# First layer of a two-layer fusion kernel: the value projection of two batches and four skip products change their place in TensorE's order

## The reference, cut to what matters

```python
def _L0_tok_ref(x, w_qkv, b_qkv, w_out, b_out):      # 16 heads of 16
    q, k, v = jnp.split(qkv, 3, axis=-1)
    logits = jnp.einsum('bhqd,bhkd->bhqk', q, k) / math.sqrt(HEAD_DIM)
    attn = jax.nn.softmax(logits, axis=-1)
    vals = jnp.einsum('bhqk,bhkd->bhqd', attn, v)
...
def _L0_attn_ref(u, A_log, D_skip, dt_proj_w, dt_proj_b, x_proj_w):   # 16 states, 589 tokens
    delta = jax.nn.softplus(jnp.einsum('blr,dr->bld', dlow, dt_proj_w) + dt_proj_b)
    h = dA * h + dB * u_t[..., None]
    y_t = jnp.sum(h * c_t[:, None, :], axis=-1)
...
    return y + u * D_skip[None, None, :]
```

## Time and profile before

| | us |
|---|---|
| median of 3 runs | 1267.5 |
| lowest and highest of them | 1264.88, 1269.35 |
| the profiled execution | 1260.33 |
| its span, first to last instruction | 1258.1 |
| share of PE, DVE, ACT, POOL busy in the span | 77%, 60%, 35%, 14% |

### The profile page before, as it was taken

One profiled execution on the slowest core, in us unless ns is written; L12 is line 12 of the kernel. 1 busy time (PEld: TensorE's weight loads), 2 busy tenths in 40 slices (PEclk: granted clock), 3 DMA queues, 4 the chain that ended last, 5 costly groups with the idle time before them and its releaser, 6 DMA issues.

```text
span 1258.1 us, 14643 instructions
## 1 busy us (share of the span) xinstructions
PE 974.3 (77%) x4854; PEld 531.5 (42%) x4855; DVE 760.9 (60%) x1321; ACT 444.4 (35%) x816; POOL 170.0 (14%) x200
## 2 busy tenths in 40 slices
PE   6999888888978889897685429998199887638880
PEld 2323332243322434234352229997066665414440
DVE  4611689975799768988799721111555657742225
ACT  1165236632366422674452113443123312302220
POOL 1000000000000000000000612333000023245550
PEclk9799899997999989899788759999599989769995
DMA  3099302300223102122233386663650000239927
GB/s 97 1 299 309 126 33 96 117 20 11 74 84 119 41 3 78 58 98 76 89 116 107 101 331 204 192 201 98 226 231 1 6 18 14 70 101 396 401 90 246
DMA packets 74058, 156.58 MB, mean 124 GB/s; under 512 B 11194, under 2 KB 55437, under 8 KB 70928
## 3 DMA queue, kind: packets, MB, share of 16 engines
q1 hardware_dynamic: 66512, 148.11, 34.5%
q0 software_dynamic: 7488, 7.70, 1.9%
HBM read 124.88 MB, written 43.69 MB: 134 GB/s over the span
## 4 chain that ended last, share of the span: by engine, by line
PE 44%; DVE 29%; issue 15%; DMA 3%; POOL 3%; ACT 3%; SPq 1%; another core or an unknown queue 1%; POOLq 0%; DVEq 0%; ACTq 0%
DVE hst L1534 10%; PE ps L594 7%; PE ps L1065 5%; DVE hC L1542 5%; PE ps L572 4%; PE ps L678 4%; PE ps L700 3%; PE ps L943 3%; DVE mxn L1483 3%; PE ps L1053 2%; PE ps L691 2%; PE ps L1013 2%; POOL ys_dram L1441 2%; PE ps L582 1%; DVE Hs L2058 1%
## 5 line engine op out<-in xcount | busy, mean ns | idle before, releaser
L700 PE MATMUL ps<-hC,ident 128*128 128x512 f32 (+1 forms) x384 | 158.1, 553 | 49.4 <-DVE hC L1542 49.4
L1483 DVE TENSOR_REDUCE mxn<-ps 128x2 f32<-128x1024 f32 x128 | 151.1, 1221 | 68.2 <-PE ps L594 67.8
L1534 DVE TENSOR_TENSOR_SCAN hst<-dA,dBu 128x1180 f32<-128x1180 f32 x64 | 167.0, 2610 | 0.5
L1145 ACT ACTIVATE Ph<-ps 128x1024 f32<-128x1024 f32 x128 | 124.1, 1022 | 85.0 <-PE ps L678 85.0
L700 PEld LDWEIGHTS ps<-hC,ident 128*128 128x128 f32 x384 | 73.8, 206 | 154.9 <-DVE hC L1542 78.7
L594 PE MATMUL ps<-Kh,Qh 32*128 32x512 f32 x512 | 110.1, 685 | 17.8 <-DVE mxn L1483 15.4
L678 PE MATMUL ps<-Qh,Kh 32*128 32x512 f32 x512 | 94.6, 663 | 8.3 <-ACT Ph L1145 8.0
L1542 DVE TENSOR_TENSOR hC<-hst,bc 128x1180 f32<-128x1180 f32 x64 | 87.2, 1366 | 8.9 <-PE ps L700 8.9
L1525 DVE TENSOR_TENSOR dBu<-dtu,bc 128x1180 f32<-128x1180 f32 x64 | 88.0, 1380 | 0.8 <-DMA bc<-bc_dram 0.7
L1425 POOL COPY xa<-home 128x20 f32<-128x20 f32 x1 | 1.2, 1165 | 613.2 <-DMA home<-in_home 613.2
L1065 PE MATMUL ps<-ring,xgT 128*64 128x256 f32 x512 | 70.1, 395 | 13.6 <-ACT xgT L1387 7.3
(11 more groups left out here) (264 smaller groups left out, 1356.8 us busy)
## 6 DMA issues: line engine op xcount, KB each, us to landing
bc<-bc_dram SPq DMA_DIRECT2D x64, 590.0 KB, 3.7
ring<-in_we SPq DMA_DIRECT2D x16, 2048.0 KB
W<-in_w SPq DMA_DIRECT2D x32, 512.0 KB
xs_dram<-zeros SPq DMA_DIRECT2D x1, 8224.0 KB, 43.0
xg<-xs_dram SPq DMA_DIRECT2D x16, 514.0 KB
yg<-ys_dram SPq DMA_DIRECT2D x12, 640.0 KB, 8.0
W<-in_w SPq DMA_DIRECT2D x7, 1024.0 KB
ys_dram<-zeros SPq DMA_DIRECT2D x1, 5120.0 KB, 48.8
```

The lines of the kernel that those rows point to most:

```text
L700: m = nc.tensor.matmul(tail[:, lo:hi], ident[:, :], state[:, lo:hi], start=False, stop=(n == NS - 1), skip_group_check=True)
L1145: nc.scalar.activation(Ph[:, n % 2, 2 * g:2 * g + 2, :], ps[:, 2 * g:2 * g + 2, :], ACT.Exp, scale=float(HD) ** -0.5).then_inc(act_p, 1)
L1483: nc.vector.tensor_reduce(slots32(mxn[:, hg % 2, i, :])[:, 2 * g:2 * g + 2, HD], ps[:, 2 * g:2 * g + 2, :], AX.X, ALU.max, negate=True).th ...
L1534: nc.vector.tensor_tensor_scan(hst[:, k % 2, :, :].rearrange("p c t -> p (c t)"), dA[:, k % 2, :, :].rearrange("p c t -> p (c t)"), dBu[:, ...
```

## The change

It does two things. `V_BEHIND` is batches 1 and 2. For these, both halves of `project_v` and of `take_v` leave the last group of the maxima stretch and stand in the scan stretch, right behind the first unit of transposed scores (on TensorE) and the first pair of exponentials (on ACT). The skip products of all four batches leave their places (for batches 0 to 2 the maxima stretch, for batch 3 the end of `back_ahead`) and stand in the second step of their scan.

```diff
+    V_BEHIND = range(1, NB - 1)
...
             def project_v(b, half):
                 if half == 0:
-                    pe.wait_ge(dve_q, HG * b + HG - 1)
+                    pe.wait_ge(dve_q, HG * (b + 1) if b in V_BEHIND else HG * b + HG - 1)
...
             def turn_maxima(b, hg):
                 pe.wait_ge(dve_max, 2 * (NU * b + QT * (hg + 1)))
-                if hg == HG - 1:
+                if hg == HG - 1 and b in V_BEHIND:
+                    pe.wait_ge(dve_q, HG * b + HG - 1)
+                elif hg == HG - 1:
                     pe.wait_ge(act_v, 2 * b + 2)
...
-                            if (hg, i) == (2, 3):
-                                skip(nb)
                         if i in (1, 2):
                             if hg + 1 < HG:
                                 project(mb, hg + 1, i - 1, 4)
-                            else:
+                            elif mb not in V_BEHIND:
                                 project_v(mb, i - 1)
...
                         tscores(eb, n)
+                        if n == 0 and eb in V_BEHIND:
+                            project_v(eb, 0)
+                            project_v(eb, 1)
                         if n:
                             weighted(eb, n - 1)
+                    if cb is not None and n == 1:
+                        skip(cb)
...
                         turn_tokens(eb, low)
+                    if n == 1:
+                        skip(cb)
                     if n >= 2:
                         add_state(cb, n - 2)
...
                 turn_y(cb)
-                skip(eb)
...
-                    take_v(mb, 0)
-                    take_v(mb, 1)
+                    if mb not in V_BEHIND:
+                        take_v(mb, 0)
+                        take_v(mb, 1)
...
                         exps(eb, n)
+                        if n == 0 and eb in V_BEHIND:
+                            take_v(eb, 0)
+                            take_v(eb, 1)
```

## The result

The changed kernel takes 1272.83 us in the median of 20 runs (1264.61 to 1279.72), the kernel before 1265.7 us in the median of 20 (1260.24 to 1272.94, and one run of 2968.02 us whose cause isn't known; the median hardly feels it). The ratio is 1.0061, with a 95% interval from 1.0043 to 1.0079: the change costs 0.6%, about 7.7 us (5.4 to 10.0). 1277.0 us against 1267.5 was forecast, a ratio of 1.0075.

The account below looks back on a forecast made before the run. No engine is full: PE weighs on the maxima stretch, DVE bounds the scan stretch, PE paces back_ahead(3, 2). 2 x 3.75 + 1.95 = +9.45 us on the 1267.5 us median gives 1277.0 us, range 1266 to 1281.

Parts of the forecast that it names:

- The values' term: Fronts and seams of batches 0 and 1: moving the values costs 3.75 us a site at the lower clock, two sites.
- The skip product's term: back_ahead(3, 2): batch 2's skip product adds 2.25 us on PE, its front gives 0.3, net +1.95 us.
- DVE takes back only what it waited, and at the lower clock nothing: front(1, 0), front(2, 1): DVE regains 1.9 us a site at full clock; lower clock adds 2 x 0.95 us of waits.
- The clock falls where scores stand alone: Last group of front(1, 0) and front(2, 1): without projections TensorE falls to 1.2 GHz, a unit taking 0.95 us more.
- skip and values keep the clock: front(2, 1), 328 to 345 us: with skip and values among the scores, the granted clock stays at 1.00.
- The chain ahead of the second scan: Seam, lower clock: turning maxima +0.45, then values, copies and decay factors make state 1's scan 3.3 us late; +3.75 a site.
- lower bound (2.95): Seam cost a site if the clock returns within the first half of the values: +2.95 us.
- 0.75 us: Seam at full clock: values, copies and decay factors make the scan of state 1 start 0.75 us late.
- At the full clock the front gives 1.9 us a site: front(1, 0), front(2, 1): DVE's waits of 0.28 and 1.76 us go, less one new gap of 0.18 us.
- back_ahead: +1.95: back_ahead(3, 2), where PE sets the pace: skip product adds 2.25 us, front gives 0.3; bounds 0 and +4.2 us.
- 0.3 us of gain: front(3, 2), where the values stay: only DVE's 0.28 us wait behind the skip product goes.
- Nothing for batch 3, SP's queue and the new waits: Batch 3's PE order, SP's later loads of x, and new waits of turn_maxima and project_v: each costs 0.

Follow-up runs that it names:

- x2: Full change with the skip products left in their old places, so only the values of batches 1 and 2 move; ratio to the kernel before 1.0061.
- x4: Full change plus unused full-row products on TensorE in the last group of the maxima stretches; ratio to the kernel before 0.9996.
- x7: Full change plus unused full-row products in the last group, and the second state's decay factors ahead of the value copies; ratio to the kernel before 1.0017.
- x1: Kernel before with only the skip products moved, all value projections left in the maxima stretch; ratio to the kernel before 0.9998.
- x3: Full change with ACT making the second state's decay factors ahead of the two value copies; ratio to the kernel before 1.0036.

## Why the prediction was right

The direction, the range and the mechanisms of the moved values held; the sum was 1.8 us too high in the median (+9.45 against +7.7), inside the interval of the measurement. The values' term agrees with their own experiment: 2 x 3.75 = 7.5 us forecast, 7.6 in x2 (4.5 to 10.8). The skip product's term has no such support, and in the one profile the two seams cost less than forecast, 4.9 us with their fronts, and front(3, 2) more. That the sum came out so near is in part luck. By its own steps:

*DVE takes back only what it waited, and at the lower clock nothing.* Right. The last group of maxima went from 13.09 to 13.31 us. The forecast was a wait of 0.95 us in each of two units; they read 1.04 and 1.05.

*The clock falls where scores stand alone.* Right at both sites, at 0.50 for 17 us. That it is the kind of product is supported by x4, whose ratio is clear of the full change's and whose profile has 1.00; x7 shows that it does not settle every execution. One reading of rows was too simple: that skip and values keep the clock (1.00 from 328 to 345). In x1, without the skip product, the clock fell ahead of the values; in x2, without the values, it fell behind the skip product. The Trainium skill's rule on idle gaps (TensorE: Matmul & The Clock Gate, section Why this matters for your kernels) does not describe this fall: the longest pause of PE in the 14 us ahead of it was 0.82 us, and PE was 84% busy with the clock at 1.00 in x4, and 86% with it at 0.50 in the changed kernel.

*The chain ahead of the second scan.* Right in kind, a little too large in size: 0.46 us for turning the maxima and 2.8 us late at the first site (3.3 in the table; 3.75 forecast), 1.9 at the second. The clock came back inside the first half of the values, which took 3.18 and 2.23 us, not 3.59, and the kernel before already had the lower clock at the second site's turn of the maxima, so that nothing was added there. The first site lies between forecast and lower bound (2.95); the second lies below the bound, which charged the turn of the maxima at both sites. x3 shows that ACT's order makes the wait. At the full clock 0.75 us was forecast; x4 measured 0.71.

*At the full clock the front gives 1.9 us a site.* Not shown as such, since only kernels with extra products kept the clock; with them (x4) the last group is 0.87 us shorter and the wait of 0.28 us ahead of it gone, 1.15 us together.

*back_ahead: +1.95.* The local reading is right, 1.3 us in the full change and 2.6 in x1. As a term of the sum it is not confirmed: x1's median shows nothing (-0.2 us, with some 3 us of room either way). What the skip product left behind in front(3, 2) was sized wrongly: I had given that front 0.3 us of gain. In the profile after it lost 6.4 us in two stretches at 0.50 that were not there before, of which one (502 to 512) begins right behind the skip's old place. The other (471 to 478) lies in the first groups, far from any edit. In x1 and x3 the clock also falls at the skip's old place (some 497 to 504), and the front takes 0.9 and 1.2 us more than before; this is nearer to what the missing product costs there, and with one profile each it is not measured well.

*Nothing for batch 3, SP's queue and the new waits.* Right: from the first scan of batch 3 to its last, 86.3 us before and after; and from the second scan of batches 0 and 1 to the first maxima of the next front 92.8 and 92.4 us, against 92.7 and 93.0 before.

## What to carry to other kernels

Before work is taken out of a stretch that another engine bounds, ask what it did there besides its result: here the projections among the scores kept TensorE at 2.4 GHz or brought it back there sooner, and without them the stretch gave back at the lower clock what it had saved. And when a producer moves, move its consumer's copy with an eye on what is queued behind it: two copies of 0.6 us, each behind its product, on an engine that is 35% busy held the bound engine for 2.8 us. Where a busy TensorE is granted the lower clock, a few full-row products in its waits can be a cheap gain (0.4 to 0.6% here). And before one profile is taken for the kernel, see where its execution lies among the runs: x4's was the fastest of twelve, x7's the slowest.

## What the runs showed of the hardware that was not expected

- The same list of TensorE gets different clocks in the same place in different executions: x4 kept 1.00 through a last group in which x7, with the same products, had 0.50 for 6.8 us. The time goes with the clock: x4's fastest run, 1234.65 us, had a mean granted clock of 0.901, and one of 1250.39 us had 0.888.
- The kernel before was paying for this already: fronts of 57.4 to 62.0 us take 56.1 with eight extra products each.
- A product of 128 rows and 256 columns of four-byte numbers takes 0.53 us of TensorE's time (1.06 a pair), more than twice the 0.21 us that I had assumed. The earlier trace rows already had it: four products of 128x256 in 1.99 us.
